# The normalised state of the gated unit is made where it is used, not stored and loaded

## The reference, cut to what matters

```python
x = x + _L0_gnn_ref(_layernorm(x), ...)          # three graph layers
x = x + _L0_ffn_ref(_layernorm(x), ...)          # experts, two of 8 for each node
x = x + _L1_gnn_ref(_layernorm(x), ...)          # the third block, below
x = x + _L1_ffn_ref(_layernorm(x), ...)          # experts, two of 16 for each node

def _L1_gnn_ref(h, relvectors, w_ih, w_hh, b_ih, b_hh, edge_src, edge_dst, edge_rel):
    msg = h[edge_src] + relvectors[edge_rel]
    red = jax.ops.segment_sum(msg, edge_dst, num_segments=h.shape[0])
    gi = red @ w_ih.T + b_ih
    gh = h @ w_hh.T + b_hh
    i_r, i_z, i_n = split(gi); h_r, h_z, h_n = split(gh)
    r = sigmoid(i_r + h_r); z = sigmoid(i_z + h_z)
    n = tanh(i_n + r * h_n)
    return (1.0 - z) * n + z * h
```

## Time and profile before

| | us |
|---|---|
| time, median of 3 runs | 1695.84 (1693.56 to 1696.71) |
| the profiled execution, its own time | 1696.88 |
| its span, first to last instruction | 1694.0 |
| PE busy | 1499.2 (89%) |
| DVE busy | 848.7 (50%) |
| ACT busy | 483.3 (29%) |
| POOL busy | 337.6 (20%) |
| mixing part of `relate` | from 1008 to 1078 |
| its sums | from 1078 to 1178 |
| `gru` | from 1181 to 1351 |

### The profile page before, as it was taken

The page is one execution under the profiler, slowest core; times in us unless marked ns, Lnnn a source line. Parts: engine busy times, 40 slices in busy tenths (PEclk is TensorE's granted clock), DMA queues, the critical chain, the costliest instruction groups (busy, mean ns, idle before and its releaser), DMA issues. The chain is left out here.

```text
span 1694.0 us, 33346 instructions
## 1 busy us (share of the span) xinstructions
PE 1499.2 (89%) x8652; PEld 1054.9 (62%) x8652; DVE 848.7 (50%) x2438; ACT 483.3 (29%) x1256; POOL 337.6 (20%) x393
## 2 busy tenths in 40 slices
PE   3796799999999999984999967899999849999966
PEld 3685664458444855544999952344666639999854
DVE  6897752333322457775222228511688852222237
ACT  2565320003000311111444433100233314444433
POOL 4000220003000310002554530000001224555430
PEclk9855899999999999995999989999999859999989
DMA  4000231123211332222223338501322245333435
GB/s 128 0 0 1 90 100 50 49 72 124 62 50 57 120 101 87 84 75 96 91 99 115 118 104 249 156 25 42 87 75 66 88 162 165 120 119 93 140 102 172
DMA packets 133643, 158.04 MB, mean 93 GB/s; under 512 B 16065, under 2 KB 118834, under 8 KB 133266
## 3 DMA queue, kind: packets, MB, share of 16 engines
q1 hardware_dynamic: 121810, 125.57, 24.0%
q0 software_dynamic: 11680, 31.61, 6.0%
q10 hardware_dynamic: 96, 0.20, 0.0%
HBM read 102.59 MB, written 57.93 MB: 95 GB/s over the span
## 5 line engine op out<-in xcount | busy, mean ns | idle before, releaser
L898 PE MATMUL layer_ps<-parts,counts 128*128 128x512 f16 x1875 | 409.1, 379 | 1.3 <-issue 0.7
L898 PEld LDWEIGHTS layer_ps<-parts,counts 128*128 (+1 forms) x1875 | 183.4, 98 | 217.7 <-issue 2.8
L1475 ACT ACTIVATE experts_hT<-experts_ps_h,experts_b_col 128x128 f32<-128x128 f32 x456 | 159.7, 368 | 99.5 <-PE experts_ps_h L1450 78.7
L1458 PE MATMUL experts_ps_y<-experts_rows,experts_hT 128*128 128x256 f32 x688 | 164.2, 381 | 0.8
L1407 POOL DMA_INDIRECT chosen<-experts_y,experts_row x116 | 114.6, 988 | 159.9 <-issue 132.9
L1458 PEld LDWEIGHTS experts_ps_y<-experts_rows,experts_hT 128*128 128x128 f32 x688 | 124.1, 190 | 16.5 <-ACT experts_hT L1475 2.9
L799 POOL TENSOR_TENSOR parts<-layer_rest,gru_rows 128x256 f32 (+2 forms) x75 | 54.5, 727 | 393.5 <-DVE layer_rest L774 393.5
L1394 POOL DMA_INDIRECT experts_fetched<-tokens,experts_index x116 | 112.2, 968 | 72.4 <-issue 44.7
L960 DVE COPY layer_total<-layer_ps 128x256 f32<-128x256 f32 x75 | 31.8, 425 | 183.3 <-PE layer_ps L898 180.4
L1450 PEld LDWEIGHTS experts_ps_h<-experts_xT,experts_rows 128*128 128x128 f32 x976 | 120.1, 194 | 4.0 <-DVE experts_xT L1491 0.9
L1450 PE MATMUL experts_ps_h<-experts_xT,experts_rows 128*128 128x128 f32 x976 | 120.6, 277 | 0.5 <-DVE experts_xT L1491 0.5
(11 more groups left out here) (321 smaller groups left out, 2036.5 us busy)
## 6 DMA issues: line engine op xcount, KB each, us to landing
experts_rows<-in_L_ffn_w SPq DMA_DIRECT2D x32, 512.0 KB, 5.1
gru_rows<-x SPq DMA_DIRECT2D x75, 128.0 KB, 2.2
own<-layer_own SPq DMA_DIRECT2D x75, 128.0 KB, 1.7
layer_own_in<-own SPq DMA_DIRECT2D x75, 128.0 KB, 2.1
h<-layer_out SPq DMA_DIRECT2D x50, 128.0 KB, 1.7
gru_rows<-h SPq DMA_DIRECT2D x50, 128.0 KB, 2.1
gru_rows<-chosen SPq DMA_DIRECT2D x25, 256.0 KB, 3.8
combine_y<-chosen SPq DMA_DIRECT2D x25, 256.0 KB, 3.4
```

The lines of the kernel that those rows point to most:

```text
L898: last = nc.tensor.matmul(ps[b][:], cst.counts[:, s, bass.ds(t * P, P)], parts[:, s, :], start=s == 0, stop=s == NT - 1)
L1458: last = nc.tensor.matmul(ps_y[:, 0:D], hT[:, c, :], down[b][:, c, :], start=c == 0, stop=c == KH - 1)
L1475: nc.scalar.activation(hT[:, c, :], ps_h[c][:, 0:P], function, bias=b1_col[:, bass.ds(e * KH + c, 1)]).then_inc(hT_ready, 1)
```

## The change

The normalised tile `hn` is still made for the sums, but it is no longer stored, and the gated unit no longer loads it. Instead:

- ACT copies the mean of each tile into a kept column `state_mean` ahead of the root, and DVE writes the inverse into a kept column `state_inverse`. Before the sums DVE makes of them the product of minus the mean and the inverse, for all tiles in one operation.
- In `gru`, ACT makes the state of a tile from `before` by one activation (Identity) with the inverse as scale and that product as bias, both pointers of 128x1. For tiles 0 to 2 it does so ahead of `copy_turned(0)`, for tile t+3 right behind the tanh of tile t. It waits for the two loads of the tile; PE's `turn` and DVE's product with the state now wait for it.
- With the store go its semaphore waits, in `norm_of` and at the end.
- To make room for the two kept columns, three small things move: `room.small` into rows of the weights' tensor, `inv_deg` as well, and `not_before` of the routing into the memory of `at_place1`.

The diff, without the last of these points:

```diff
@@ -1559,18 +1561,12 @@
                     sp.dma_start(x[b], dr.x1[rows(t), :]).then_inc(got[b], 16)
                     sp.dma_start(y[b], dr.both_choices[rows(t)]).then_inc(got[b], 16)
 
-                def store_normed(u, b):
-                    sp.wait_ge(normed, u + 1)
-                    sp.dma_start(dr.hn[rows(u), :], hn[b % 2][:]).then_inc(hn_stored[b % 2], 16)
-
                 def step(k, b):
                     t = k * B + b
                     sp.wait_ge(taken, t + 1)
                     sp.dma_start(dr.x2[rows(t), :], out[b % 2][:]).then_inc(stored[b % 2], 16)
                     if not past(t + B):
                         load(t + B, b)
-                    if not early(t - 1):
-                        store_normed(t - 1, b + 1)
 
                 def store_sums(t, k, b, bank):
                     sp.wait_ge(red_ready, t + 1)
@@ -1579,12 +1575,10 @@
                 for b in range(B):
                     load(b, b)
                 tile_loop(sp, step, n=B, ahead=B, behind=2)
-                store_normed(NT - 1, NT - 1)
                 load_gru_rows(sp, ins, cst, w_rows)
                 sums_loop(sp, store_sums)
                 for b in range(2):
                     sp.wait_ge(stored[b], 16 * uses(b))
-                    sp.wait_ge(hn_stored[b], 16 * uses(b))
                     sp.wait_ge(red_stored[b], 16 * uses(b))
 
...
@@ -1652,6 +1646,7 @@
                     if not early(t - 2):
                         low(t - 2, b)
                     act.wait_ge(var_ready, t + 1)
+                    nc.scalar.copy(cst.state_mean[:, bass.ds(t, 1)], small[b % 2][:, 6:7])
                     norm_root(nc, cst, small[b % 2]).then_inc(std_ready, 1)
 
                 loop(act, step)
@@ -1661,15 +1656,13 @@
 
             @block.vector
             def _(dve):
-                def norm_of(u, use, b):
-                    if not early(u - 2):
-                        dve.wait_ge(hn_stored[b], use * 16)
-                    nc.vector.tensor_scalar(hn[b][:], out[b][:], small[b][:, 6:7], small[b][:, 9:10], ALU.subtract,
-                                            ALU.mult).then_inc(normed, 1)
+                def norm_of(u, b):
+                    nc.vector.tensor_scalar(hn[b][:], out[b][:], small[b][:, 6:7], cst.state_inverse[:, bass.ds(u, 1)],
+                                            ALU.subtract, ALU.mult).then_inc(normed, 1)
 
                 def inverse_of(u, b):
                     dve.wait_ge(std_ready, u + 1)
-                    nc.vector.reciprocal(small[b][:, 9:10], small[b][:, 8:9]).then_inc(inverted, 1)
+                    nc.vector.reciprocal(cst.state_inverse[:, bass.ds(u, 1)], small[b][:, 8:9]).then_inc(inverted, 1)
 
                 def remain(u, b):
...
@@ -1705,10 +1698,10 @@
                     nc.vector.bn_aggr(small[d][:, 6:8], small[d][:, 0:6]).then_inc(var_ready, 1)
 
                 loop(dve, step)
-                u, use, d = NT - 1, (NT - 1) // 2, (NT - 1) % 2
+                u, d = NT - 1, (NT - 1) % 2
                 inverse_of(u, d)
                 dve.drain()
-                norm_of(u, use, d)
+                norm_of(u, d)
                 remain(NT - 2, 1 - d)
                 dve.drain()
                 dve.wait_ge(rels_ready, 1)
@@ -1726,6 +1719,9 @@
                     nc.vector.scalar_tensor_tensor(out[b][:], ps[bank][:, D:2 * D], 1.0 / LO_SCALE, mixed[b][:], ALU.mult,
                                                    ALU.add).then_inc(red_ready, 1)
 
+                dve.drain()
+                dve.wait_ge(std_ready, NT)
+                nc.vector.scalar_tensor_tensor(cst.state_mean[:], cst.state_mean[:], -1.0, cst.state_inverse[:], ALU.mult, ALU.mult)
                 dve.drain()
                 sums_loop(dve, keep_sums)
...
@@ -1910,6 +1906,7 @@
             return wT[:, i, :, g * P:(g + 1) * P], w_banks[n % len(w_banks)][:, 0:D].rearrange("p (c d) -> p c d", c=KD)
 
         loaded = [sem(f"loaded{b}") for b in range(B)]
+        state_ready = sem("state_ready")
         turned, xT_ready, product = sem("turned"), sem("xT_ready"), sem("product")
         pre_ready, gate_ready, cand_ready, new_ready, used = (sem("pre_ready"), sem("gate_ready"), sem("cand_ready"),
...
@@ -1943,7 +1940,6 @@
                     if not at_start(k):
                         sp.wait_ge(used, t - (B - 1))
                     sp.dma_start(x[b][0][:], sums[rows(t), :]).then_inc(loaded[b], 16)
-                    sp.dma_start(x[b][1][:], states[rows(t), :]).then_inc(loaded[b], 16)
                     sp.dma_start(before[b][:], source[rows(t), :]).then_inc(loaded[b], 16)
                     if at_start(k) and b == 1:
                         for i, n in enumerate(("L1_gnn_b_ih", "L1_gnn_b_hh")):
@@ -1973,7 +1969,8 @@
                     pe.wait_ge(done, GC)
 
                 def turn(b, loads):
-                    pe.wait_ge(loaded[b], loads * 48)
+                    pe.wait_ge(loaded[b], loads * 32)
+                    pe.wait_ge(state_ready, loads * B - (B - 1 - b))
                     for i in range(2):
                         for c in range(KD):
                             last = nc.tensor.transpose(ps_t[b % 2][:, i, c, :], x[b][i][:, c * P:(c + 1) * P], cst.ident[:])
@@ -2043,6 +2040,11 @@
                     act.wait_ge(w_turned, n + 1)
                     nc.scalar.copy(*chunk(n)).then_inc(w_ready[0], 1)
 
+                def normalise_state(t, b, loads):
+                    act.wait_ge(loaded[b], loads * 32)
+                    nc.scalar.activation(x[b][1][:], before[b][:], ACT.Identity, scale=cst.state_inverse[:, bass.ds(t, 1)],
+                                         bias=cst.state_mean[:, bass.ds(t, 1)]).then_inc(state_ready, 1)
+
                 def copy_turned(t, d):
                     act.wait_ge(turned, t + 1)
                     nc.scalar.copy(xT[d][:], ps_t[d][:]).then_inc(xT_ready, 1)
@@ -2073,6 +2075,8 @@
                             copy_token(u, u)
                     act.wait_ge(cand_ready, t + 1)
                     nc.scalar.activation(new[d][:], cand[d][:], ACT.Tanh).then_inc(new_ready, 1)
+                    if not past(t + B - 1):
+                        normalise_state(t + B - 1, (b + B - 1) % B, k + 1 + (b + B - 1) // B)
 
                 def beside(t):
                     if t in (PART_A + 1, PART_B + 1):
@@ -2083,6 +2087,8 @@
                     for u in together:
                         copy_token(u, together[-1])
 
+                for b in range(B - 1):
+                    normalise_state(b, b, 1)
                 copy_turned(0, 0)
                 loop(act, step)
                 nc.scalar.preload_act_table(ACT.Sqrt)
@@ -2126,7 +2132,7 @@
                         finish(t - 1, 1 - d)
                     dve.wait_ge(gate_ready, t + 1)
                     nc.vector.tensor_tensor(hidden[d][:], hidden[d][:], gate[d][:, 0:D], ALU.mult)
-                    dve.wait_ge(loaded[b], (k + 1) * 48)
+                    dve.wait_ge(state_ready, t + 1)
                     nc.vector.tensor_tensor(saved[d][:], gate[d][:, D:2 * D], x[b][1][:], ALU.mult)
                     dve.drain()
                     nc.vector.tensor_tensor(cand[d][:], cand[d][:], hidden[d][:], ALU.add).then_inc(cand_ready, 1)
@@ -2187,7 +2193,7 @@
     dr = Scratch()
     dr.x0, dr.x1, dr.x2 = (scratch(f"x{i}", NP) for i in range(3))
     dr.h1, dr.h2 = scratch("h1", NP), scratch("h2", NP)
-    dr.own, dr.hn, dr.red = scratch("own", NP), scratch("hn", NP), scratch("red", NP)
+    dr.own, dr.red = scratch("own", NP), scratch("red", NP)
     dr.packed = nc.dram_tensor("packed", [N_EDGES + 2 * P, 1], I32, kind="Internal").ap()
     dr.tokens, dr.chosen = scratch("tokens", NP), scratch("chosen", 2 * NP + P)
     dr.both_choices = dr.chosen[0:2 * NP, :].rearrange("(c n) d -> n c d", c=2)
@@ -2197,11 +2203,12 @@
         cst.semaphores = Semaphores(nc)
         cst.ident, cst.ones, cst.before = sb("ident", [P, P]), sb("ones", [P, P]), sb("before", [P, P])
         cst.eps = sb("eps", [P, 1])
+        cst.state_inverse, cst.state_mean = sb("state_inverse", [P, NT]), sb("state_mean", [P, NT])
         w_rows = sb("gru_rows", [P, 2, 3 * KD, D])
         with ExitStack() as graph:
             gb = lambda n, s, d=F32: graph.enter_context(nc.sbuf_tensor(n, s, d))
             cst.counts = gb("counts", [P, NT, NP], F16)
-            cst.inv_deg = gb("inv_deg", [P, NT])
+            cst.inv_deg = w_rows[:, 1, KD * 2, 100:100 + NT]
             E0 = ins["L0_ffn_Wr"].shape[1]
             logit0 = gb("logit0", [P, NT, E0])
             if True:
@@ -2246,7 +2253,7 @@
             tokens = mix.enter_context(nc.sbuf_tensor("tokens1", [P, NT, D], F32))
             logit1 = mix.enter_context(nc.sbuf_tensor("logit1", [P, NT, E1], F32))
             choice = Choice(mix, nc, "choice1_", E1)
-            gru(nc, ins, cst, dr, w_rows, dr.red, dr.hn, dr.x2, x3, stats3, E1, ins["L1_ffn_gate_w"], ins["L1_ffn_gate_b"],
```

(1 more changed line is left out.)

18 lines of the change are left out of this document (10 added, 8 removed).

## The result

The changed kernel takes 1697.14 us, the median of 22 runs (1695.20 to 1700.03). The kernel before, run beside it, takes 1694.45 (22 runs, 1690.85 to 1698.86). The ratio is 1.0016 with an interval of 1.0011 to 1.0022: +2.7 us, from +1.9 to +3.7. The forecast was +2.5, and 1698.4 as the time; it stands 1.3 too high mainly because the three runs of the kernel before that it started from had a median of 1695.84, and the 22 have 1694.45. The likeliest case, no change by 0.2%, is what happened.

A forecast was written before the change was run, and what follows sets the result against it. VectorE's order was taken to pace the mixing part, TensorE to bound the sums and `gru`. -0.4 - 3.9 + 4.3 + 2.5 = +2.5 us on 1696.88 gave 1699.4, or 1698.4 as median; range 1692.5 to 1703.5.

The forecast's parts named there:

- Part 1: Mixing part of `relate`: store wait goes, gain 2.4; mean's copy delays the root, cost 2.0; net -0.4 us, -3.2 to +4.0.
- the gain: Mixing part: `norm_of` no longer waits for the old store, five waits, 2.4 us in all.
- 0.8 either way: Mixing part: the reciprocal's t-dependent address and the removed wait's register work taken as even, 0.05 x 16 us.
- Part 2: Sums: weights' loads issued 2.3 us earlier shrink TensorE's pause and spare the low clock; -3.9 us, 0 to -5.0.
- the low clock behind the pause: Sums: 3.3 us of work at half rate after TensorE's pause, 1.6 us lost before, assumed to go.
- Part 3: Start of `gru`: TensorE's first product 2.7 us later, waiting for tile 2's state, plus 1.6 low clock; +4.3 us, 0 to +7.4.
- the rival with 0.22: First tiles of `gru`: clock stays low for 6.0 us of work, 3.0 lost in place of 1.6; time 1701.4; chance 0.22.
- both of my bounds: Start of `gru`: low-clock loss between 0 (clock doesn't fall) and 3.0 us (6.0 us of work at half rate).
- Part 4: Loop of `gru`: state of 0.49 us between tanh and copy of t+2 lengthens tiles; +2.5 us, +1.3 to +3.3.
- The late store: Sums: first store of a sum is late anyway, so no gain there; time 1702.3; chance 0.14.
- Tile 2 in time: Start of `gru`: tile 2's loads come in time, ACT never waits, clock never falls; 1694.1 or 1692.1; chance 0.16.
- The table: `gru`: ACT reloads its activation table for every state, +32 us, about 1730; chance 0.03.

The follow-up runs named there:

- early weights: Kernel before, with SP issuing the gated unit's two weights' loads ahead of the last two `hn` stores: 1691.11 us, 0.9985 of the kernel before.
- experiment 5: Gated unit's weights' loads issued ahead of the last two `hn` stores in the kernel before: 1691.11 us, 0.9985; after the last norm in the changed kernel: 1699.23, 1.0034.
- experiment 3: Changed kernel with the state of tile t+3 made behind the sigmoid of tile t, not behind the tanh: 1697.80 us, 1.0002 of the kernel before.
- the changed kernel again: The changed kernel, unedited, measured a second time in another comparison: 1694.66 us, 1.0008 of the kernel before.
- experiment 7: Changed kernel with the state of tile t+3 made behind the copy of turned tile t+2, not ahead of it: 1698.50 us, 1.0042 of the kernel before.
- experiment 2: Changed kernel with tile 2's state made behind the second copy of a turned tile, not ahead of the first: 1696.23 us, 0.9987 of the kernel before.

## Why the prediction came out, step by step

**Part 1 (forecast -0.4, found about +0.5).** With the copy out of the way the stage is 67.56 to 68.71 in four executions, mean 68.06; with it ahead of the root 69.70 to 70.97 in seven, mean 70.5; before, 69.94. But its first tiles wait for loads for a time that varies, and one stretch is sharper: from the fifth reciprocal to the last, twenty steps, it repeats within 0.02 us. It takes 52.47 with the copy ahead of the root, 50.94 with it behind, and 51.64 in the kernel before (51.77 with early weights). So the copy costs 1.5 us in twenty steps, where 20 x 0.10 were forecast for all: a tile is 0.09 longer (2.31 for 2.22), but in the loop only three tiles in four are. That term was about right. The term that was mis-sized is the gain. Four of the five waits for the store lay in this stretch, 1.4 us, and 0.7 came back. In the first fifteen of the steps nothing did (39.72 before, 39.81 with the copy behind the root), although two of those waits went, 0.86 us; they are these rows of the kernel before:

```profile
1051.48 0.41 DVE L1667 TENSOR_SCALAR relate_hn<-relate_out,relate_small 128x256 f32<-128x256 f32 x1 [0.38 <-DMA hn<-relate_hn]
...
1062.38 0.41 DVE L1667 TENSOR_SCALAR relate_hn<-relate_out,relate_small 128x256 f32<-128x256 f32 x1 [0.48 <-DMA hn<-relate_hn]
```

Something of about that size took their place, and the prediction had set such costs as even (0.8 either way). What shows is that the reciprocal waits for the root 9 times, 2.4 us, even with the copy behind it, and once before. Whether that is the register work of its address or ACT's additional instruction is not told apart.

**Part 2 (forecast -3.9, found -4.5).** Right in its mechanism for the larger part: experiment 5 has it both ways. The loads went out 0.38 behind the last store of `out`, where the first of the two `hn` stores had stood, and so 6.43 us ahead of the sums' second part (1073.36 to 1079.79). Before, it was 4.07 (1077.20 to 1081.27): 2.36 earlier, forecast 2.3. The wait for the first store shrank by 2.74, 0.4 more than that, and the pause to 0.52 and not 1.1. By experiment 5 the earlier place alone leaves a pause of 1.83, so 1.3 of the 2.85 us by which it shrank belong to the missing stores, which the forecast had not counted. The 1.6 us for the low clock behind the pause went too, as taken: the slice from 1092 to 1093 has 1.00.

**Part 3 (forecast +4.3, found +2.3 to +6.1).** The wait was there, of the size that was named: the first product came 10.34 us after the first turned weights, not 7.26, +3.1 for a forecast of +2.7. The load of tile 2's `before` is this row of the changed kernel's DMA issues, 1179.3 to 1179.6:

```profile
gru_before<-x SPq DMA_DIRECT2D x1, 128.0 KB, 5.5
```

It gained 0.4 by the lighter traffic, where I took 0.3, but only 0.9 by its earlier issue, where I took 1.4: SP issued it 3.74 us behind the first turned weights (1175.58 to 1179.32), before 4.62 (1181.59 to 1186.21). The clock after this pause was mis-sized in the profiled execution, which lost 3.0 and not 1.6; that is the rival with 0.22. Over the seven executions that have the pause unfilled, it cost 3.0, 2.6, 1.7, 2.9, 0, 1.6 and 2.6: mean 2.1, with both of my bounds reached. Neither the forecast nor the rival was the rule. The first product of the kernel of experiment 3, and of the changed kernel again:

```profile
1186.74 3.70 PE L1988 MATMUL gru_ps_g<-gru_wT,gru_xT 128*128 128x512 f32 x8 [2.71 <-ACT gru_xT L2050]
```

```profile
1185.12 6.35 PE L1988 MATMUL gru_ps_g<-gru_wT,gru_xT 128*128 128x512 f32 x8 [2.83 <-ACT gru_xT L2050]
```

The seven pauses are 2.71 to 4.19 us long. The shortest cost nothing and the next, 0.12 longer, 2.6; the longest but one, 3.88, cost 1.6. So their length does not order the losses; whether the shortest was spared by its length or by chance, and what sets the rest, stays open; that the pause makes them at all is shown by experiment 7, and what makes the pause by experiment 2.

**Part 4 (forecast +2.5, found +2.9).** The price of the state, x = 0.49, was right to the hundredth. The mechanism was half of the truth. I had the copy of t+2 queued behind the state and did not look at who waits for the state itself. TensorE's turn of t+3 does, ahead of those same products, and its path is equally long. It cost nothing for the forecast, because the two tie, but it would have misled a repair: the obvious one, state behind copy, costs 3.0 more (experiment 7), where by the prediction's path it should have taken the loss away. The size came out 0.4 higher than forecast. The eight tiles of the loop lost 2.0 (forecast 1.9), so 0.3 of it lies in the tiles written out; how much of that is the turn's is not told apart.

**The rivals.** The late store fell (its wait went from 4.46 to 1.72, and experiment 5 moved it with the loads). Tile 2 in time fell (ACT waited 3.84). The table fell: from 1177 to 1347 the changed kernel loads it five times, each 1.28 us, at the places written for it, and none of them at a state.

The Trainium skill (ScalarE: Activation LUTs, What ACT_TABLE_LOAD costs) gave 0.585 us for a state by its rule of 186 ns, 0.833 ns per element and 93 ns for each pointer operand; the trace has 0.587. For a copy of 128x1 the same rule would give 0.187, an estimate, and the trace has 0.174 to 0.178. The same page (Table sets: the hidden batching unit) has Identity in every set, and the trace agrees: none of the loads stands at a state.

**The sum.** +0.5 (mixing, means of executions) - 4.5 + 3.1 + 2.1 (start of `gru`, wait and clock) + 2.9 = +4.1, where many runs measured +2.7 [+1.9, +3.7]. The forecast of +2.5 owes something to luck: parts 1, 3 and 4 were each low by 0.4 to 0.9, part 2 was short of its gain by 0.6, and the sum of what was found is 1.4 above what many runs measured. That last gap need not be a mechanism. In the thirteen profiled executions of the other kernels the four stages less the total run from -2.9 to +2.7 us, and their mean is +0.2 (last two columns of the table), all against one execution of the kernel before. A single profile places a cost to the tenth within a stage, and gives the total to some 3 us.

## What to carry to other kernels

A small operation that is put on an engine with time to spare costs by its place in that engine's order: ask for each instruction queued behind it, and for each engine that waits on its own result, when it was last early enough. Here three such places, moved without removing any work, turned +2.7 us (+1.4 the second time) into -6.1. And look at what a removed transfer let pass in its queue: the one stage that gained, 4.5 us, gained 3.1 of them by two unrelated loads that moved up by 2.4 us, and the kernel before gets those (2.5 us in its total) with its traffic unchanged.

## What was unexpected of the hardware

After pauses of TensorE of 2.71 to 4.19 us the granted clock fell in six executions and not in the seventh: the loss was 3.0 us after the longest, 1.6 after 3.88, 2.6 after 2.83, and 0 after the shortest, in the kernel of experiment 3. Filling the pause with four products kept it at 1.00. A load of 128 KB took 5.5 us behind 768 KB of broadcast rows, and a store of 128 KB took 4.9 behind the two weights' loads but 2.3 when these had been issued 2.4 us earlier.
